# Second attention: a new order within a step, fillers, and the last two images divided on VectorE

## The reference

```python
h = wavelet_mix(x); h = concatenate([h, txt], axis=1)
h = h + attn0(layernorm(h));  h = h + moe0(layernorm(h))
h = h + attn1(layernorm(h));  h = h + moe1(layernorm(h))

def attn1(x):          # 16 heads of 16 in 4 groups that share keys and values
    q = (x @ Wq.T + bq).reshape(b, n, G, hpg, HD); k, v = ...
    scores = einsum('bqghd,bkgd->bghqk', q, k) / sqrt(HD)
    y = einsum('bghqk,bkgd->bqghd', softmax(scores), v)
    return y.reshape(b, n, d) @ Wo.T + bo
```

## Time and profile before

| | us |
|---|---|
| median of 3 runs | 837.94 |
| the three runs | 836.92, 837.94, 849.18 |
| the profiled execution | 837.31 |
| its span | 835.5 |
| PE busy | 745.6 (89%) |
| DVE busy | 566.7 (68%) |
| ACT busy | 340.1 (41%) |
| mean granted TensorE clock | 0.958 |

### The profile page before, as it was taken

How to read it: one execution, slowest core, us unless ns; L and a number is a source line. 1 busy time by engine, 2 the same in 40 slices (tenths; PEclk the granted TensorE clock), 3 DMA queues, 4 the chain that set the end, 5 groups by cost and what they waited for, 6 DMA issues and landing times.

```text
span 835.5 us, 13547 instructions
## 1 busy us (share of the span) xinstructions
PE 745.6 (89%) x4928; PEld 605.8 (73%) x4928; DVE 566.7 (68%) x1213; ACT 340.1 (41%) x598; POOL 130.5 (16%) x124
## 2 busy tenths in 40 slices
PE   4639995799999999499999999889798999999997
PEld 4528994599999999375444444332566999999997
DVE  6295777677777777817666666652587677777776
ACT  1305444423333333312676777666324233333332
POOL 0105554000000000052102452222330000000000
PEclk9999998989999999689999999986899999999999
DMA  7210000000000000054446545400500000000000
GB/s 250 100 71 1 1 0 1 1 1 1 1 2 2 0 0 0 1 138 98 58 102 115 101 95 101 62 17 22 201 0 1 1 21 15 5 20 11 10 20 20
DMA packets 21641, 34.82 MB, mean 42 GB/s; under 512 B 6612, under 2 KB 17540, under 8 KB 21072
## 3 DMA queue, kind: packets, MB, share of 16 engines
q1 hardware_dynamic: 16136, 31.06, 14.3%
q10 hardware_dynamic: 5448, 3.01, 2.2%
HBM read 24.03 MB, written 9.99 MB: 41 GB/s over the span
## 4 chain that ended last, share of the span: by engine, by line
PE 81%; DVE 12%; issue 2%; ACT 2%; DMA 1%; SPq 0%; POOL 0%; ACTq 0%; DVEq 0%; POOLq 0%
PE PS L1215 17%; PE PS L1217 17%; PE PS L1216 16%; PE PS L1471 7%; PE PS L1455 5%; PE PS L1446 5%; PE PS L1223 2%; DVE MX L1128 2%; PE PS L1555 2%; PE PS L1244 2%; PE PS L1479 1%; PE PS L1337 1%; PE PS L1303 1%; PE PS L1235 1%; DMA halves<-in_halves 1%
## 5 line engine op out<-in xcount | busy, mean ns | idle before, releaser
L1128 DVE TENSOR_REDUCE MX<-PS 128x2 f32<-128x576 f32 x144 | 108.9, 756 | 64.7 <-PE PS L1455 63.6
L1054 DVE SCALAR_TENSOR_TENSOR h<-PS,cmb,h 128x256 f32<-128x256 f32 (+1 forms) x342 | 143.9, 477 | 0.2 <-PE PS L1217 0.2
L666 ACT ACTIVATE PR<-PS 96x768 f32<-96x768 f32 x144 | 115.2, 807 | 52.9 <-PE PS L1446 51.9
L608 ACT ACTIVATE sg<-PS 128x384 f32<-128x384 f32 x114 | 56.1, 492 | 165.8 <-PE PS L1217 165.8
L1039 DVE TENSOR_TENSOR al<-aa,ah 128x384 fp32r<-128x384 f32 x114 | 63.7, 559 | 67.0 <-ACT ah L612 67.0
L612 ACT ACTIVATE ah<-aa 128x384 fp32r<-128x384 f32 x114 | 59.8, 525 | 83.7 <-DVE aa L1033 83.7
L1033 DVE TENSOR_TENSOR aa<-sg,PS 128x384 f32<-128x384 f32 x114 | 63.2, 554 | 26.6 <-ACT sg L608 26.1
L1215 PE MATMUL PS<-xTh,W1h 128*128 128x384 f32 x240 | 80.9, 337 | 0.0
L1216 PE MATMUL PS<-xTh,W1l 128*128 128x384 f32 x240 | 80.7, 336 | 0.0
L1217 PE MATMUL PS<-xTl,W1h 128*128 128x384 f32 x240 | 80.6, 336 | 0.0
L1471 PE MATMUL PS<-PR,VA 128*32 128x288 f32 x768 | 71.8, 451 | 3.6 <-ACT yr L704 3.6
(11 more groups left out here) (234 smaller groups left out, 1551.6 us busy)
## 6 DMA issues: line engine op xcount, KB each, us to landing
QS<-scrH SPq DMA_DIRECT2D x30, 144.0 KB, 4.3
W1raw<-in_w SPq DMA_DIRECT2D x1, 3840.0 KB, 12.1
W0raw<-in_w SPq DMA_DIRECT2D x1, 3456.0 KB, 10.8
scrH<-qh SPq DMA_DIRECT2D x8, 432.0 KB, 2.5
scrL<-ql SPq DMA_DIRECT2D x8, 432.0 KB, 3.1
out_tokens<-h SPq DMA_DIRECT2D x6, 384.0 KB, 2.3
QS<-scrL SPq DMA_DIRECT2D x15, 144.0 KB, 4.9
x_in<-in_x SPq DMA_DIRECT2D x2, 1024.0 KB, 6.2
```

The costliest lines, as they stand in the source:

```text
L666: A_(PR[0:KT, ca:cb + 1:cb - ca, :], PS[0:KT, b:b + 2, 0:CW], ACT.Exp).then_inc(s["e_exp"], 1)
L1054: ins = V.scalar_tensor_tensor(out=hj, in0=PS[:, b + t // 2, (t % 2) * D:(t % 2) * D + D], scalar=cmb[:, ds(g * GT + t, 1), e:e + 1].squee ...
L1128: V.tensor_reduce(MX[:, hf, z:z + NSH // 2 + 1:NSH // 2], PS[:, b:b + 2, 0:POS], AX_X, ALU.max).then_inc(s["e_mx"], 1)
```

## The change

Five things, all in the second attention:

1. On PE the row scores of a step are issued ahead of its transposed scores; before it was the other way round.
2. The last two images (`NLATE = 2`, images 6 and 7) are divided by PE and DVE, at the places of the list `LATE` (turn offset, U), in two banks, 4 and 5 in turn. Image 6's sums and reciprocals no longer go through DRAM, POOL divides images 0 to 5, and the eight transfers on ACT's queue at the end of turn 9 are gone.
3. Fillers: in turn 8 four each at U = 7, 12, 16; in turn 9 from U = 4 on one in steps 9, 10, 11, 13, 14, 15 and three in the others.
4. `warm_up(6)` in place of `warm_up(3)` ahead of the output projection.
5. SP waits for the inverses of six images and not of seven before it loads W1.

```diff
-        sp.wait_ge(s["e_rb"], 16 * 2 * HPG * (IMGS - 1))
+        sp.wait_ge(s["e_rb"], 16 * 2 * HPG * (IMGS - NLATE))
...
-            if it == IMGS + 1:
-                for n in range(len(RB_U)):
-                    inverses_in(IMGS - 2, n)
...
-                for n in last_at(it, U):
+                for c in late_at(it, U):
+                    i, n = late(c)
                     g = Y_G[n]
...
-                    dve.wait_ge(s["e_sb"], n + 1)
-                    own(V.reciprocal(b, PS[:, 7, 0:POS]))
+                    dve.wait_ge(s["e_sb"], c + 1)
+                    own(V.reciprocal(b, PS[:, 4 + c % 2, 0:POS]))
...
         def turn(it):
             for U in range(NU):
                 keep_busy(busy_at(it, U))
-                if live(it, 2):
-                    i = it - 2
-                    ...
-                    wait(pe, s["e_exp"], i * NU + U - 1)
-                    scores(i, U)
                 k, c = s_at(U)
                 if live(it, k):
                     i = it - k
...
                     wait(pe, s["e_mx"], NSH * i + c - (1 if early(it) else 0))
                     row_scores(i, c, max_bank(it, c))
+                if live(it, 2):
+                    i = it - 2
+                    ...
+                    wait(pe, s["e_exp"], i * NU + U - 1)
+                    scores(i, U)
...
+                for c in late_at(it, U):
+                    i, n = late(c)
+                    pe.wait_ge(s["e_yr"], NGQ * i + n + 1)
+                    if c == 0:
+                        pe.wait_ge(s["e_mx"], NSH * IMGS)
+                    if c >= 2:
+                        pe.wait_ge(s["e_yl"], late_done(c - 2))
+                    M(PS[:, 4 + c % 2, 0:POS], spread[:, Y_G[n] % 2], yr[i % 3][:, Y_G[n]], start=True, stop=True).then_inc(s["e_sb"], 1)
...
+                if it >= IMGS:
+                    if late_busy(it, U):
+                        wait_misc()
+                    keep_busy(late_busy(it, U), 7)
...
-        warm_up(3)
-        pe.wait_ge(s["e_yt"], NGQ // 2 * (IMGS - 1))
-        pe.wait_ge(s["e_yl"], NGQ + 2)
+        warm_up(6)
+        pe.wait_ge(s["e_yt"], NGQ // 2 * (IMGS - NLATE))
+        pe.wait_ge(s["e_yl"], (NGQ + 2) * NLATE)
...
+NLATE = 2
+LATE = [(0, 4), (0, 7), (0, 10), (0, 13), (0, 16), (1, 0), (1, 4), (1, 8)]
...
+def late_busy(it, U):
+    if it == IMGS:
+        return 4 if U in PR_U else 0
+    return (1 if U in AV_U else 3) if it == IMGS + 1 and U > MT_U[1] else 0
```

More of the change, by code:

```diff
@@ L480, in _ @@
                 low_halves(it + 1)
-            if live(it, 4) and not last_image(it - 4):
+            if live(it, 4) and not late_image(it - 4):
                 divide(it - 4)
@@ L485, in _ @@
                     nc.gpsimd.tensor_tensor(h[:, j, :], h[:, j, :], bo1[:, :], ALU.add).then_inc(s["e_bo"], 1)
-        pool.wait_ge(s["e_yl"], NGQ + 2)
+        pool.wait_ge(s["e_yl"], (NGQ + 2) * NLATE)
         n1 = sum(WCOLS[1]) // NG
@@ L668, in turn @@
                     high_part(it + 1, PR_U.index(U - 1))
-                if live(it, 3) and not last_image(it - 3):
+                if live(it, 3) and not late_image(it - 3):
                     i = it - 3
@@ L684, in turn @@
                         act.dma_start(scrR[i].rearrange("h g q -> (h g q)").rearrange("(p c) -> p c", c=SW), rec[:, :]).then_inc(s["e_ro"], 16)
-                if live(it, 4) and not last_image(it - 4) and U in RB_U and it < IMGS + 2:
+                if live(it, 4) and not late_image(it - 4) and U in RB_U:
                     inverses_in(it - 4, RB_U.index(U))
-            if it == IMGS + 1:
-                for n in range(len(RB_U)):
-                    inverses_in(IMGS - 2, n)
         def inverses_in(i, n):
@@ L1136, in turn @@
                     V.tensor_tensor(Ml[:, b], PS[0:NSH, 7, 0:P], Mh[:, b].bitcast(F32), ALU.subtract).then_inc(s["e_msplit"], 1)
-                if U == REC_U and live(it, 3) and not last_image(it - 3):
+                if U == REC_U and live(it, 3) and not late_image(it - 3):
                     i = it - 3
@@ L1142, in turn @@
                     V.reciprocal(rec[:, :], sm[:, :]).then_inc(s["e_rec"], 1)
-                for n in last_at(it, U):
+                for c in late_at(it, U):
+                    i, n = late(c)
                     g = Y_G[n]
                     b = (qf[0][:, 0], qf[0][:, 1], qf[0][:, 2], qf[1][:, 0])[g]
-                    if n == 0:
+                    if c == 0:
                         dve.wait_ge(s["e_split"], 3 * IMGS)
-                    dve.wait_ge(s["e_sb"], n + 1)
-                    own(V.reciprocal(b, PS[:, 7, 0:POS]))
+                    dve.wait_ge(s["e_sb"], c + 1)
+                    own(V.reciprocal(b, PS[:, 4 + c % 2, 0:POS]))
                     own.settle()
-                    dve.wait_ge(s["e_yr"], NGQ * (IMGS - 1) + n + 1)
-                    V.scalar_tensor_tensor(out=b, in0=yr[(IMGS - 1) % 3][:, g], scalar=halves[:, g % 2:g % 2 + 1], in1=b, op0=ALU.mult, op1=ALU.mult)\
+                    dve.wait_ge(s["e_yr"], NGQ * i + n + 1)
+                    V.scalar_tensor_tensor(out=b, in0=yr[i % 3][:, g], scalar=halves[:, g % 2:g % 2 + 1], in1=b, op0=ALU.mult, op1=ALU.mult)\
                         .then_inc(s["e_yl"], 1)
@@ L1156, in turn @@
                         a = (qf[0][:, 0], qf[0][:, 2])[g // 2]
-                        dve.wait_ge(s["e_yl"], n + 1 + g // 2)
-                        V.tensor_tensor(img(yT[:, g // 2, :], IMGS - 1), a.rearrange("p (j c) -> p j c", j=NT), b.rearrange("p (j c) -> p j c", j=NT), ALU.add)\
+                        dve.wait_ge(s["e_yl"], late_done(c) - 1)
+                        V.tensor_tensor(img(yT[:, g // 2, :], i), a.rearrange("p (j c) -> p j c", j=NT), b.rearrange("p (j c) -> p j c", j=NT), ALU.add)\
                             .then_inc(s["e_yl"], 1)
@@ L1483, in turn @@
                 keep_busy(busy_at(it, U))
+                k, c = s_at(U)
+                if live(it, k):
+                    i = it - k
+                    if c == 0:
+                        for a in range(2):
+                            pe.wait_ge(s[f"e_in{a + 2 * (i % 2)}"], 16 * 6 * (i // 2 + 1))
+                        if i == 0:
+                            pe.wait_ge(s["e_prev"], 6)
+                    wait(pe, s["e_mx"], NSH * i + c - (1 if early(it) else 0))
+                    row_scores(i, c, max_bank(it, c))
                 if live(it, 2):
@@ L1495, in turn @@
                     scores(i, U)
[L1496 to L1505, removed]
                 for k, n, kt in av_at(U):
@@ L1633, in values_done, with late_image, late, late_at @@
     return i * NAV + z // NKT * 2 * NKT + a * NKT + z % NKT + 1
[L1636 to L1644, removed]
+def late_image(i):
+    return i >= IMGS - NLATE
+def late(c):
+    i, n = divmod(c, NGQ)
+    return IMGS - NLATE + i, n
+def late_at(it, U):
+    return [c for c in range(NLATE * NGQ) if LATE[c] == (it - IMGS - 1, U)]
+def late_done(c):
+    i, n = divmod(c, NGQ)
+    return (NGQ + 2) * i + (1, 2, 4, 6)[n]
+def late_busy(it, U):
+    if it == IMGS:
+        return 4 if U in PR_U else 0
+    return (1 if U in AV_U else 3) if it == IMGS + 1 and U > MT_U[1] else 0
 def early(it):
```

## The result

| | before | after |
|---|---|---|
| median of 20 runs each | 838.94 us | 845.71 us |
| lowest, highest | 830.56, 850.16 | 841.52, 864.55 |
| ratio, 95% interval | | 1.0095 [1.0073, 1.0116] |
| the profiled execution, its span | 837.31, 835.5 | 846.35, 844.5 |
| mean granted TensorE clock | 0.958 | 0.957 |

The ratios here leave out runs in which a kernel was disturbed, while the medians take all of them, so a ratio and two medians can differ a little. By the ratio the change costs 8.0 us (0.0095 x 838.94), by the medians 6.8. The forecast was 839.3, +1.4. The time is within 2% of before, and slower for certain.

What follows compares the result with a forecast made beforehand. It took the chain row score, maximum, row score between PE and DVE, 1.26 us a step, to pace the loop. Swap +3.7, fillers +0.6, new end -2.9 made +1.4, so 839.3 us, range 832 to 846.

Steps and rivals of the forecast that it cites:

- The swap in plain steps: Second attention, steps with nothing displaced: DVE's 1.26 us a step decides, so the new order changes nothing.
- The swap's displaced steps: Turns 2 to 8: scores now delay the projections and the transpose of the maxima on PE, +3.7 us.
- The upper bound of +4.4: Displaced steps of turns 2 to 8: the swap's cost if each displaced step costs 0.30 us.
- Fillers in turn 8: Turn 8, U = 7, 12, 16: four fillers each lengthen three steps without values by 0.2, +0.6 us (0 to 0.9).
- The new end: Turn 9's first row scores to the output projection: 36.1 us against 38.97, -2.9 us (-5.8 to -0.5).
- W1's load and casts: End of turn 9: they move forward but weren't on the path, hidden by the projection; worth nothing.
- The clock: Turns 9 and 10: premise that fillers in turn 8's holes keep the clock at 1.00.
- rival B: Turn 7 or 8: the clock falls inside it, +10 us, up to 848; chance 0.12.
- Rival A: Second attention: the swap is free and fillers are cheap, 0 and -5.8 us, 832.1; chance 0.22.
- C: Turns 9 and 10: the clock stays at 0.50 and the new work costs double, 865 us; chance 0.06.

Runs made afterwards that it cites:

- e6: e3 with the projection and the transpose of the maxima moved to right behind the row scores; 833.86 us, ratio 0.9902.
- e3: The changed kernel plus three fillers each at U = 17 of turns 2 to 8 and U = 7, 12, 16 of turn 7; 836.02 us.
- e4: e2 with the same added fillers as e3; 833.35 us, ratio 0.9920.
- e5: The kernel before, old order and old end, with e3's added fillers and four at U = 7, 12, 16 of turn 8; 831.89 us, ratio 0.9887.
- e8: e4 without turn 9's fillers, turn 8's kept; 829.03 us, ratio 0.9862.
- e1: The kernel before with only the swap, row scores ahead of the scores; 851.86 us, ratio 1.0146.
- e2: The changed kernel with the old order of scores and row scores, so the new end and its fillers alone; 838.91 us, ratio 0.9991.
- e9: The changed kernel plus three fillers each at U = 7, 12, 16, 17 of turn 7 and U = 17 of turn 8; 838.09 us, ratio 1.0010.
- e12: e6 without the fillers of turn 9; 830.63 us, ratio 0.9945.
- e10: The changed kernel plus three fillers at U = 17 of turns 2 to 6 alone; 843.13 us, ratio 1.0116.
- e11: e8 with only the transpose of the maxima moved to right behind the row scores; 826.66 us, ratio 0.9879.

## Why the prediction was wrong, point by point

**The swap in plain steps: nothing.** Right. Row scores follow each other by 1.25 to 1.26 us there, as before.

**The swap's displaced steps: +3.7.** Right in mechanism (e6 takes it away), too large in size: 2.6 in the ledger, 2.7 between e3 and e4. Turn 6 lost 0.43 and not 0.69: 0.12 around U = 7 (forecast 0.22), 0.12 around U = 11 and 12 (0.25), 0.18 around U = 16 (0.22); in turn 7 the transpose at U = 11 cost 0.18. The upper bound of +4.4 doesn't follow from its own words either: 17 displaced steps at 0.30, less 0.24, are 4.9. One of the mis-sized terms is the projection's start, taken as 0.56 behind the row scores. Turn 6 after, around U = 7, on PE and DVE, which answers to the earlier trace rows:

```profile
507.36 0.40 PE L1452 MATMUL PS<-KS,QS 48*128 48x288 f32 x2
507.59 0.34 PE L1443 MATMUL PS<-QS,KS 50*96 50x384 f32 x2
507.86 0.41 PE L1212 MATMUL PS<-xTh,a1h 128*128 128x288 f32 x1
508.88 0.40 PE L1452 MATMUL PS<-KS,QS 48*128 48x288 f32 x2
508.99 0.52 DVE L1111 TENSOR_SCALAR qf<-PS,bq 128x288 f32<-128x288 f32 x1 [0.43 <-PE PS L1214]
509.43 0.75 DVE L1124 TENSOR_REDUCE MX<-PS 128x2 f32<-128x576 f32 x1
```

The scores start 0.23 behind the row scores and the projection 0.27 behind the scores, 0.50 in all. The maximum is 2.07 behind the row scores of U = 7: 1.94 before, 2.16 forecast.

**Fillers in turn 8: +0.6.** Right: +0.50, from 0.14, 0.23 and 0.13 in three steps.

**The new end: -2.9.** Near: -3.55. Turn 9 takes 24.84 (25.6 forecast) and the projection starts 35.42 behind the first row scores (36.1 forecast), at clock 1.00 throughout, as forecast. The eight transfers for image 6 are gone and so is PE's wait of 3.65, but ACT's queue isn't free of transfers in turn 9, against what the prediction expected to see: the eight for image 5 are issued there, from 574.98 to 586.27, one at a time. In turn 10 there are none. DVE's last division and the six warm-up products end together, and the projection follows:

```profile
601.46 0.75 PE L1524 MATMUL PS<-yr,spread 128*128 128x288 f32 x2 [0.53 <-ACT yr L700]
602.05 4.03 PE L1220 MATMUL PS<-same_img,ones 128*128 128x384 f32 x12
605.32 0.46 DVE L1155 TENSOR_TENSOR yT<-qf,qf 128x288 f32<-128x288 f32 x1
605.93 15.78 PE L1557 MATMUL PS<-wo,yT 128*128 128x256 f32 x72
```

But it is near by luck. The prediction had PE's 3.65 us among what the new end takes away and compared its 36.1 at clock 1.00 with a 38.97 of which 27 us were at 0.50. The gain was the clock's: held, the old end takes 32.84 with those 3.65 in it (e5), and the new one is 2.3 longer (e4). What makes it so are turn 9's fillers, 4.6 us (e8); the forecast had 8 x 0.7 + 6 x 0.36 = 7.8 us of them in its 25.6 and didn't ask what turn 9 would be without. A small slip beside it: by its own row a warm-up product is 7.90 / 24 x 2 = 0.66 and not 0.645.

**W1's load and casts: nothing.** Right. From the projection's start to the end both kernels take 238.6.

**The clock. This is the step that failed.** The sum took the price of the old fall as gained and set nothing for a new one, "The clock is the premise", and gave a fall inside the turns (rival B) a chance of 0.12. B is what happened, though the largest fall came in turn 4 and not in 7 or 8: 10.5 us here, as B's +10 had it. The swap makes it worse: it brings 37 us of half clock more by itself (e1) and 14 on top of the new end (e2, after). It isn't the swap alone, since e2's profile falls in turns 7 and 8 in the old order. The prediction looked at what the swap does to each instruction's start and not at what it does to PE's holes. A likely mechanism, argued from the order and the busy shares: before, the scores filled part of the wait for the maximum, which the row scores had to sit out anyway; with the row scores in front PE idles through all of it (1.01 at the start of a turn, 0.85 before), and the scores follow without a gap. The trace of before had a sign: turn 8, PE busy 19.76 of 22.80, ended in a fall, and turn 7 looked the same; the prediction said so and priced it as one rival in eight.

**Rival A,** that the swap is free and fillers are cheap, was wrong on both its counts: the swap costs 2.6 at full clock, and turn 9's fillers cost 4.6. **C** didn't occur in turns 9 and 10 of the kernel after. e1, the swap without fillers there, shows a clock that stays down through turns 8 and 9, 48 us, but not C's doubled price of the new work, which e1 doesn't have.

The median of 845.71 lies at the upper end of the range, and by B's mechanism, not by the forecast's. With the measured terms and that of the new falls the same sum gives 837.94 + 2.6 + 0.5 - 3.5 + 10.5 = 848.0.

**What stays open.** What the new end is worth against the old one at clock 1.00 in both, and with it how much of the 8.0 us is there with the clock held: 4.1 or 8.1, by medians or by ratios. What the chip's monitor of PE's activity answers to isn't shown: only that fillers in the holes stop most of the falls and that the new order brings more time at half clock. Why single runs of e6, e9 and e12 still fell, and why turn 4 fell in the profiled execution and turn 6 didn't with the same holes, is open as well. The share of the loss that lies in turns 7 and 8 rests on e9 and e10 and their intervals, 7 us of some 9.

## What to carry to other kernels

Where the engine has to wait in each step, keep the work that is ready ahead of the instruction that waits: a swap may leave a plain step's length as it is and still bring the clock down (e1: 1.5%). Sum a change at full clock and at half clock apart (here a third of a microsecond for each one at half clock), and before a gain is credited to a removed wait, work out what that stretch takes at clock 1.00. A filler belongs where the trace shows TensorE idle: three in each of the short holes took 9 us off, thirty in turn 9, where PE was busy throughout, cost 4.6.

## What the runs showed of the hardware

**Half clock lasts though the records are nearly gapless.** In the kernel after the clock fell at 440.3 and stayed down for some 24 us, with PE's records busy 31.05 of turn 4's 32.62; in e1 it stayed down for 48 us with 45.04 busy.

**DVE's addition grows six times as long beside POOL.** Turn 9 after, on DVE and POOL; the same instruction at 605.32 (above) takes 0.46:

```profile
588.28 2.79 DVE L1155 TENSOR_TENSOR yT<-qf 128x288 f32<-128x288 f32 x1
588.04 2.71 POOL L472 TENSOR_TENSOR recb<-yr,recb 128x1152 f32<-128x1152 f32 x1 [20.32 <-DMA recb<-scrR]
```

It lasted 2.79 us and ended 0.3 behind POOL's multiplication. The same pair stands in the profiles of e2, e3, e4, e8 and e11, each time with DVE's addition starting 0.15 to 0.35 behind POOL and lasting 2.78 to 2.80. In e8 PE then waits 1.22 us for DVE, at 577.58. The Trainium skill (SBUF — State Buffer, SBUF: two separate sides) says that a DVE instruction with two inputs in SBUF and a GpSimd one that reads SBUF take a shared pair of ports in turn, each for its whole length. The traces agree: here 0.46 + 2.33 of waiting, against the 2.47 that POOL had left.
